# Differential attention and gated feed-forward on one core: the sums turned in 32x32 blocks by VectorE

## What is computed

```python
q1, q2, k1, k2 = (heads(x @ W) for W in (Wq1, Wq2, Wk1, Wk2))    # 2 x 16 heads x 2048 x 16
v = heads(x @ Wv)                                                # 2 x 16 heads x 2048 x 32
a1 = softmax(where(causal, q1 @ k1.T * scale, -inf))
a2 = softmax(where(causal, q2 @ k2.T * scale, -inf))
out = (a1 - lam * a2) @ v                                        # lam: one number for a head
merged = (layernorm(out, of each head) * (1 - LAM_INIT)).transpose(...).reshape(B, S, 512)
x = layernorm(x + merged @ Wo)
h = silu(x @ w1.T * s1) * (x @ w2.T * s2)                        # 1024 wide
h = gelu(h @ h1.T * hs1); h = gelu(h @ h2.T * hs2)
x = layernorm(x + h @ w3.T * s3)
```

## Time and profile before

| | us |
|---|---|
| runs | 1883.39 (median), 1882.99, 1884.66 |
| span of the profiled execution | 1880.4 |
| heads 0 to 14 | 939 |
| last head, to the first layer of the feed-forward | 73 |
| from there to the end | 720 |

### The profile page before, as it was taken

The page is one execution under the profiler, slowest core; times in us unless marked ns, Lnnn a source line. Parts: engine busy times, 40 slices in busy tenths (PEclk is TensorE's granted clock), DMA queues, the critical chain, the costliest instruction groups (busy, mean ns, idle before and its releaser), DMA issues.

```text
span 1880.4 us, 30846 instructions
## 1 busy us (share of the span) xinstructions
PE 1850.4 (98%) x12172; PEld 1060.4 (56%) x12172; DVE 1035.6 (55%) x2005; ACT 1408.3 (75%) x1702; POOL 229.5 (12%) x308
## 2 busy tenths in 40 slices
PE   8999999999999999999999999999999999999997
PEld 6774333333333333333333335888888888888886
DVE  5566566556655665566556655454545454636343
ACT  5549999999999999999999997454545454544452
POOL 3002111211121112111211121000000000000000
PEclk9999999999999999999999999999999999999999
DMA  8777634663466346634663411000010100000000
GB/s 270 263 259 163 113 67 78 116 111 64 82 115 116 59 82 116 116 63 78 116 104 73 80 53 43 26 12 34 12 34 12 34 12 34 12 34 23 1 12 14
DMA packets 130673, 146.11 MB, mean 78 GB/s; under 512 B 74756, under 2 KB 100996, under 8 KB 122884
## 3 DMA queue, kind: packets, MB, share of 16 engines
q1 hardware_dynamic: 128936, 139.32, 33.8%
q10 hardware_dynamic: 1584, 4.72, 0.7%
HBM read 101.79 MB, written 39.06 MB: 75 GB/s over the span
## 4 chain that ended last, share of the span: by engine, by line
PE 92%; DVE 5%; issue 1%; DMA 0%; ACT 0%; SPq 0%; DVEq 0%; PEldq 0%
PE attn_sums_ps L1104 27%; PE split_hid_ps L1716 25%; PE attn_s_ps L1079 20%; PE split_hid_ps L1700 6%; PE proj_qk_ps L545 3%; PE split_y_ps L1733 3%; PE proj_v_ps L555 2%; PE split_y_ps L1656 2%; PE attn_sums_ps L1112 2%; PE split_turn_ps L1644 1%; DVE attn_raw L1252 1%; DVE attn_raw L1241 1%; DVE attn_sums_sb L1236 0%; DVE attn_diff L1261 0%; DVE proj_xt_low L424 0%
## 5 line engine op out<-in xcount | busy, mean ns | idle before, releaser
L1041 ACT ACTIVATE attn_probs<-attn_s_ps 128x1024 f32<-128x1024 f32 x1088 | 1002.5, 1122 | 6.9 <-PE attn_s_ps L1079 6.3
L1104 PE MATMUL attn_sums_ps<-attn_probs,heads_v 128*32 128x512 f32 (+3 forms) x5120 | 586.3, 539 | 0.1
L1079 PEld LDWEIGHTS attn_s_ps<-heads_q,heads_k 50*128 50x128 f32 x2560 | 211.7, 184 | 434.5 <-ACT attn_probs L1041 376.6
L1079 PE MATMUL attn_s_ps<-heads_q,heads_k 50*128 50x512 f32 (+3 forms) x2560 | 449.7, 426 | 0.0
L1810 ACT ACTIVATE split_whole<-split_hid_ps,scales 128x512 f32<-128x512 f32 x128 | 88.3, 690 | 274.3 <-PE split_hid_ps L1716 274.1
L1022 POOL TENSOR_SCALAR_AFFINE_SELECT attn_probs<-attn_probs 128x512 f32<-128x512 f32 x256 | 176.7, 702 | 832.2 <-ACT attn_probs L1041 832.2
L1716 PE MATMUL split_hid_ps<-split_hid_b,ffn_r 128*128 128x512 f32 x1024 | 240.8, 392 | 0.0
L1716 PE MATMUL split_hid_ps<-split_hid_a,ffn_r 128*128 128x512 f32 x1024 | 237.9, 391 | 0.0
L1716 PEld LDWEIGHTS split_hid_ps<-split_hid_a,ffn_r 128*128 128x128 f32 x1024 | 190.0, 188 | 41.0 <-DVE split_hid_a L1985 1.3
L1716 PEld LDWEIGHTS split_hid_ps<-split_hid_b,ffn_r 128*128 128x128 f32 x1024 | 189.8, 188 | 38.2
L1104 PEld LDWEIGHTS attn_sums_ps<-attn_probs,heads_v 128*32 128x32 f32 x5120 | 107.6, 108 | 174.0 <-issue 139.3
(11 more groups left out here) (182 smaller groups left out, 1682.0 us busy)
## 6 DMA issues: line engine op xcount, KB each, us to landing
heads_q_raw<-qk_raw SPq DMA_DIRECT2D x60, 384.0 KB
heads_k_raw<-qk_raw SPq DMA_DIRECT2D x60, 384.0 KB
qk_raw<-proj_copies SPq DMA_DIRECT2D x64, 256.0 KB, 2.5
values<-proj_v SPq DMA_DIRECT2D x8, 1024.0 KB, 6.5
heads_k_raw<-ones SPq DMA_DIRECT2D x60, 128.0 KB
heads_v<-values SPq DMA_DIRECT2D x15, 512.0 KB, 19.0
heads_spare<-in_ffn SPq DMA_DIRECT2D x30, 256.0 KB, 9.7
split_heads<-diffs SPq DMA_DIRECT2D x7, 1024.0 KB, 5.2
```

The costliest lines, as they stand in the source:

```text
L1041: nc.scalar.activation(weights, side_by_side, ACT.Exp, scale=SCALE).then_inc(exp_done, 1)
L1079: last = nc.tensor.matmul(s_ps[(NU * h + n) % SLOTS][:, s, col:col + width], k_sb[u][rows, b * SEQ + j * PARTS:b * SEQ + (j + 1) * PARTS], ...
L1104: last = nc.tensor.matmul(sums[c * D:(c + 1) * D, off:TILE], v_sb[u][:, b * KEY_BLOCKS + j, :], probs[k % PROBS][:, b, s, place:place + wi ...
```

## The change

Both softmaxes of a batch now stand side by side in the bank: softmax s has columns 256*s to 256*s + 255. The four partition groups are c = 2*batch + r, where r is the parity of a query's group of 32. So a 32x32 block of the bank is 32 elements by 32 queries, and DVE's block transpose reads the bank and writes `raw` with queries in partitions; partition p = 64*batch + 32*r + i. `copy_sums`, `turn`, `sums_sb` and the waits on them are gone; `take_sums` is in their place. `diff` holds a batch in 64 partitions, and SP's stores and their pattern follow.

For each block, `weigh` has 8 matmuls with half the columns where it had 4, and it takes its columns from the probabilities in runs of 32 with a step of 64.

With that layout, the squares for the first 512 queries can't be taken from `diff` as before: they are taken in the last head from `early["heads"]`. POOL squares the 15 known heads in four parts after the masks of step 9, DVE sums each (`sum_known`), and each part waits for the sum of the part ahead (one buffer, `known_square`). Head 15's part goes to DRAM and back (`store_first`, and a load of 128x4x32), and `early_var` waits for it. `early_wo` stands ahead of these. `late` is now `finish_tile` alone, since `take_sums` of the last tile stands at the end of `last_head`.

```diff
@@ attention_programs @@
-    TURN_LAG = 2
...
+    HALF_TILE = TILE // 2
+    GROUPS = TILE // (2 * D)
+    ROWS = BATCH * D
...
+        SQUARES_AT = END[1]
@@ sync_program @@
-            def store_rows(h, rows, done):
-
+            def store_rows(h, b, begin, end, done):
+
+                to = diffs[b * KEY_BLOCKS:(b + 1) * KEY_BLOCKS, :, h, :].rearrange("k (g p) n -> p (k g) n", p=ROWS)
+                sp.dma_start(to[:, begin:end, :], diff[b * ROWS:(b + 1) * ROWS, begin:end, :]).then_inc(done, 16)
+
+            def store_first(h):
+
+                sp.wait_ge(diff_ready, NT * h + 1)
+                store_rows(h, 0, 0, GROUPS, first_stored)
...
+                    store_first(h)
+                    sp.wait_ge(first_stored, 16)
+                    sp.dma_start(early["heads"][:, :, KNOWN:KNOWN + D], diffs[0:SUBS].rearrange("s p h d -> p s (h d)")[:, :, KNOWN:KNOWN + D]).then_inc(heads_whole, 16)
@@ gpsimd_program @@
+                    if h == LAST and k == SQUARES_AT:
+
+                        pool.wait_ge(heads_in, 16)
+                        for s in range(SUBS):
+                            pool.wait_ge(known_summed, s + 1)
+                            known = early["heads"][:, s, 0:KNOWN].rearrange("p (h d) -> p h d", d=D)
+                            pool.tensor_tensor(known_square[:, :, :], known, known, ALU.mult).then_inc(known_squared, 1)
@@ weigh @@
                 for j, off, width, place in laid(k):
-                    for b in range(BATCH):
-                        for s in range(2):
-                            c = 2 * b + s
-                            last = nc.tensor.matmul(sums[c * D:(c + 1) * D, off:TILE], v_sb[u][:, b * KEY_BLOCKS + j, :], probs[k % PROBS][:, b, s, place:place + width],
-                                                    start=(j == 0), stop=(k == END[t] and j == blocks[-1]))
+                    for s in range(2):
+                        for b in range(BATCH):
+                            alternate = probs[k % PROBS][:, b, s, place:place + width].rearrange("p (g r n) -> p g r n", r=2, n=D)
+                            for r in range(2):
+                                c = 2 * b + r
+                                last = nc.tensor.matmul(sums[c * D:(c + 1) * D, s * HALF_TILE + off // 2:(s + 1) * HALF_TILE], v_sb[u][:, b * KEY_BLOCKS + j, :],
+                                                        alternate[:, :, r, :], start=(j == 0 and s == 0), stop=(k == END[t] and j == blocks[-1] and s == 1))
                 last.then_inc(probs_free, 1)
-
-            def turn(h, t):
...
@@ vector_program @@
-            def copy_sums(h, t):
-                n = NT * h + t
+            def take_sums(h, t):
 
                 dve.wait_ge(probs_free, PROBS + NS * h + END[t] + 1)
-                dve.wait_ge(turned, n + 1)
-                nc.vector.tensor_copy(sums_sb[:, :], sums_ps[t % 2][:, :]).then_inc(sums_copied, 1)
-
-            def take_turned(h, t):
-                n = NT * h + t
-                dve.wait_ge(turned, n + 2)
-                nc.vector.tensor_copy(raw[:, :, :, :].rearrange("p k s d -> p (k s d)"), sums_ps[t % 2][:, :]).then_inc(sums_bank_free, 1)
+                nc.vector.transpose(raw[:, :, :, :].rearrange("p s g d -> p (s g d)"), sums_ps[t % 2][:, :]).then_inc(sums_bank_free, 1)
...
+            def sum_known(s):
+
+                dve.wait_ge(known_squared, s + 1)
+                nc.vector.tensor_reduce(head_var[:, :].rearrange("p (s h) -> p s h", h=HEADS)[:, s, 0:LAST], known_square[:, :, :], AXIS.X, ALU.add).then_inc(known_summed, 1)
 
             def early_var():
 
-                nc.vector.tensor_copy(early["heads"][:, :, KNOWN:KNOWN + D], early_rows()).then_inc(heads_whole, 1)
-                dve.wait_ge(head_summed, HEADS)
+                dve.wait_ge(heads_whole, 16)
+                newest = early["heads"][:, :, KNOWN:KNOWN + D]
+                nc.vector.tensor_tensor(head_square[:, :, :], newest, newest, ALU.mult).then_inc(last_squared, 1)
...
                 tile(h, 0)
-                square_heads(h)
+                early_wo()
+                for s in range(SUBS):
+                    sum_known(s)
                 early_var()
-                early_wo()
-                copy_sums(h, 1)
                 early_rstd()
                 early_norm(0)
                 early_norm(1)
-                take_turned(h, 1)
-                finish_tile(h, 1)
+                tile(h, 1)
```

More of the change, by code:

```diff
@@ L999, in head @@
                 load_half(2 * h)
-                store_ahead(h)
+                store_ahead(h, last)
                 load_half(2 * h + 1)
@@ L1155, in use @@
                 weigh(h, u, k)
-                if k - TURN_LAG in END:
-                    turn(h, END.index(k - TURN_LAG))
-                elif k - TURN_LAG + NS in END and not first:
-                    turn(h - 1, END.index(k - TURN_LAG + NS))
                 if h == LAST:
@@ L1178, in tensor_program @@
             use(LAST, LAST % 2, False, NS - 1)
-            def late():
-                turn(LAST, NT - 1)
-            if_wide(pe, wide, "tensor", late, late, lambda: pe.wait_ge(wide_loaded, 16 * CHUNKS))
+            if_wide(pe, wide, "tensor", None, no_part, lambda: pe.wait_ge(wide_loaded, 16 * CHUNKS))
         def vector_program(dve, exact):
@@ L1245, in finish_tile @@
                 v0 = VEC * n
-                rows = diff[:, SUBS * BATCH * t:SUBS * BATCH * (t + 1), :]
-                sums = raw[:, :, :, :].rearrange("p k s d -> p (k s) d")
+                rows = diff[:, GROUPS * t:GROUPS * (t + 1), :]
+                sums = raw[:, :, :, :].rearrange("p s g d -> p (s g) d")
                 dve.wait_ge(sums_bank_free, 2 + n + 1)
@@ L1260, in finish_tile @@
                     dve.wait_ge(stored, STORES * h + STORES)
-                nc.vector.scalar_tensor_tensor(rows[:, :, 0:D - 1], raw[:, :, 1, 0:D - 1], keep["neg_lam"][:, bass.ts(h, 1)], raw[:, :, 0, 0:D - 1], ALU.mult, ALU.add).then_inc(vec, 1)
+                nc.vector.scalar_tensor_tensor(rows[:, :, 0:D - 1], raw[:, 1, :, 0:D - 1], keep["neg_lam"][:, bass.ts(h, 1)], raw[:, 0, :, 0:D - 1], ALU.mult, ALU.add).then_inc(vec, 1)
                 dve.wait_ge(vec, v0 + 3)
@@ L1390, in last_head @@
                     early_add(s)
-                copy_sums(h, 2)
-                take_turned(h, 2)
+                take_sums(h, 2)
                 early_heads(2)
@@ L1402, in last_head, with late @@
                 early_xt(1)
-                copy_sums(h, 3)
-            def late(part):
-                if part == 0:
-                    take_turned(LAST, NT - 1)
-                else:
-                    finish_tile(LAST, NT - 1)
-            def late_all():
-                late(0)
-                late(1)
+                take_sums(h, NT - 1)
+            def late():
+                finish_tile(LAST, NT - 1)
             def rest_of_first():
@@ L1689, in tile @@
                 pair = hid_ps[2 * (m % 2):2 * (m % 2) + 2]
-                if split and not prior and m == 2:
-                    late()
                 if m < 2:
@@ L1987, in tile @@
             if split and not prior:
-                late(1)
+                late()
             for layer, hid in enumerate((hid_b, hid_a)):
```

62 lines of the change are left out of this document (25 added, 37 removed).

## The result

| | runs, us | median | ratio to before |
|---|---|---|---|
| before | 1882.99 to 1884.66 | 1883.36 | |
| after | 1915.53 to 1928.7 | 1924.11 | 1.021 (1.020 to 1.023) |

The kernel became 2.1% slower (1.020 to 1.023), and the time lies far beyond the range of 1877.8 to 1890 us. The runs also scatter over 13 us, where those of before stay within 1.7.

A forecast was written before the change was run, and what follows sets the result against it. ACT's exponentials were taken to bound heads 0 to 14, PE the last head's end and the feed-forward. Terms of -4.4 + 0 + 4.2 - 0.4 = -0.6 us against 1883.39 us gave 1882.8 us, range 1877.8 to 1890.

The forecast's parts named there:

- Twice the matmuls, with half the columns: `weigh` in heads 0 to 14: PE's small extra time stays hidden behind ACT's exponentials, so 0 us.
- loads wholly exposed: Upper bound for the doubled matmuls of `weigh`: PE's weight loads not hidden, up to 1974 us.
- The extra 0.18 us a pair: `weigh` pairs: groups have 64 columns, so weight loads decide the time, adding about 0.18 us a pair.
- rival 1: PE becomes the bound in every head: 1974 us in full (chance 0.05), about 1890 us in part (0.09).
- the turns' -4.4 us: Heads 0 to 14: dropping PE's turns gives back 0.31 us a head in 14 heads, plus 0.1 for two copies.
- rival 2: The head's 0.31 us does not come back, being due to narrow steps, not turns: 1887.2 us, chance 0.08.
- The feed-forward's -0.4 us: Feed-forward: the last turn goes, with the slower restart behind it, saving 0.4 us.
- The last head's +4.2 us: Last head: PE's waits for POOL and DVE, less a saved turn, plus longer pairs and steps, add 4.2 us.
- The rounds: Last head: POOL's four squares, each waiting for DVE's sum of the one ahead, take 6.2 us in all.
- The first wait: Last head: PE waits some 2.3 us for POOL's mask of step 11; a second, before `turn_heads(0)`, takes 3.2 us.
- rival 4: Last head: waits are longer and the granted clock could fall to 1.2 GHz, about 1886 to 1889 us, chance 0.10.
- rival 3: The last head costs less, as POOL and DVE alternate faster or PE regains the wait: 1877.4 us, chance 0.18.

The follow-up runs named there:

- run 1: The kernel before, with each matmul of `weigh` cut into two of half the columns and nothing else changed: 1915.54 us, ratio 1.016.
- run 2: The changed kernel with one matmul for both softmaxes, so 4 matmuls a block instead of 8, same layout and strided reading: 1888.95 us, ratio 1.003.
- run 8: As run 4, but with eight matmuls a block in the fourth tile of each head alone, after the loads: 1877.3 us, ratio 0.997.
- run 5: The changed kernel with the known heads' squares on DVE and SP's 16 loads for the next head handed out two per two steps: 1877.06 us, ratio 0.997.
- run 4: The changed kernel with both one matmul for both softmaxes (4 a block) and the known heads' squares on DVE: 1877.14 us, ratio 0.9967.

## Why the prediction was wrong

**The step that failed** is the term "Twice the matmuls, with half the columns", which the sum has at 0 in heads 0 to 14. It priced how long PE needs for the matmuls, and never that 40% more matmuls (12172 to 17036 on the page), each with its weight load, have to be brought to PE as well. The real term is +40.0 us in the profiled execution, and 31 to 35 us in the medians. The upper bound, "loads wholly exposed", was one of PE's execution too, so the range could not hold the result. The signs were there before: q8 on the page, a DMA share of 0.51 and 0.53 as the mean of a head, and in the DMA view of before from 335 to 372 us, slices of nine tenths and more for 24 of the 37 us. Runs 1, 2 and 8 settle the count, and run 5 the loads.

**Its price of PE was right.** The prediction gave a full `weigh` 1.00 us and 0.215 us between groups. It is 1.00 us (300.86 to 301.86), and groups start 0.216 us apart. The extra 0.18 us a pair was too much: a pair takes 1.01 us (357.50 to 358.51), and its groups of 64 columns start 0.056 us apart, so the loads are hidden even there. So rival 1 is out in either size. The sign that was named for it, ACT with idle time in a middle head, did show, but its cause is another. Out for this case is also the rule of the Trainium skill, page "TensorE: Matmul & The Clock Gate", section "Part 3: Packing small matmuls — row/col tiling", that stood beside it in the prediction: weight loads overlapped here with matmuls though they use the same rows.

**Right as well:** the turns' -4.4 us (-4.6 in heads 1 to 14 of runs 2 and 4: 62.33 a head against 62.65), so rival 2 is out; the block transpose at 0.7 us (0.717 us, the mean of 64, where the figure of the Trainium skill, page "VectorE: DVE Perf Modes", section "The three transpose paths", gave an estimate of 1.24), hidden in heads 0 to 14; head 15's way through DRAM, hidden. The feed-forward's -0.4 us can't be told: from the last exponential to the end it takes 723.5 to 724.1 us in the four kernels with the turn, and 723.3 to 723.9 in the six without.

**The last head's +4.2 us was mis-sized**: +11.1. The rounds are right (1.75 us against 1.73), but the list of what stands ahead of them lacks POOL's 7.0 us. The prediction read the earlier trace rows for how long POOL's operations take, not for what stands between two of different kinds. The first wait is 9.3 us, and it hides the second (3.2 predicted, none seen), since DVE is done when PE, at half the clock, gets to `turn_heads(0)` at 1161.29. The fall of the clock in such a wait is the mechanism of rival 4, to which the prediction gave one chance in ten; it had priced the waits at 2.3 and 3.2 us.

**The decision itself** would have come out differently with the two facts: the idea is sound, as run 4 shows (-6.5 us in the medians; 4.6 of it are the turns and 1.0 is the last head, in the profiled executions), and only two details of its form cost 47 us. With neither of them, 1877.1 us is about what rival 3, no wait in the last head, was priced at (1877.4).

## What to carry to other kernels

Count an engine's instructions as well as their time: where they are cut finer while bursts of loads fill the DMA engines, the blocks of instructions can come late, so merge what one instruction can do (a pattern with one more dimension) or hand the loads out in portions. A change of POOL's kind of operation can be work of its own, 6 to 7 us here ahead of the first product and of the first all-reduce behind it; look in the trace for the instruction that marks it, put it where POOL is idle anyway, or give the work to another engine. Pauses that end in "issue", and runs of one kernel that scatter over 13 us where those of before stay within 1.7, are the signs of the first.

## What the runs showed of the hardware

- PE's instructions come through a DMA queue in packets of 16 KB, 256 instructions. Each packet took 1.2 us in the mean of heads 1 to 14, and PE restarted 1.4 to 1.65 us after the end of the one it waited for. With the DMA engines up to half busy the packet started at most 3.8 us after PE's start on the block ahead, in the traces of before and after, and with more load on them up to 10.5 us after it.
- At six of seven pauses of PE of 1.6 to 2.8 us the granted clock fell to half for 3.4 to 6.8 us; at one of 2.2 us it did not. Around a wait of 9.3 us it was at half for 13.65 us, from 3.4 us into the wait on. What the shorter pauses of one head add to that was not tried.
- POOL stood still for 6.9 to 7.0 us ahead of a product after masks, for 128x64 as for 128x480, and for 5.8 us ahead of the first all-reduce behind a product. A mask after a product, and an all-reduce after masks alone, started at once.
- An operand that PE reads in runs of 32 elements with a step of 64 costs what a contiguous one does: 1.00 us for 2048 columns in 8 or 16 instructions.
- DVE's block transpose of 128x512 from the bank took 0.717 us, against 0.68 us for a copy of the same.
